# Attention on one core: the score matmul is issued before the matmul of the maximum pass in each sub-slot

## What is computed

```python
qkv = x @ attn_qkvw + attn_qkvb              # x is the layernormed input
scores = jnp.einsum('bhqd,bhkd->bhqk', q, k) * scale
probs = jax.nn.softmax(scores, axis=-1)
ctx = jnp.einsum('bhqk,bhkd->bhqd', probs, v)
```

## Time and profile before

| | |
|---|---|
| median of 3 timed runs | 3867.29 us |
| the three runs | 3867.56, 3867.29, 3861.1 us |
| time of the profiled execution | 3863.99 us |
| span of its trace | 3862.3 us |
| busy share of the span: PE, DVE, ACT, POOL | 86%, 63%, 45%, 43% |
| granted TensorE clock, mean | 0.952 |

### The profile page before, as it was taken

One profiled execution on the slowest core, in us unless ns is written; L12 is line 12 of the kernel. 1 busy time (PEld: TensorE's weight loads), 2 busy tenths in 40 slices (PEclk: granted clock), 3 DMA queues, 4 the chain that ended last, 5 costly groups with the idle time before them and its releaser, 6 DMA issues. The chain is left out here.

```text
span 3862.3 us, 66576 instructions
## 1 busy us (share of the span) xinstructions
PE 3336.4 (86%) x25168; PEld 1740.8 (45%) x25168; DVE 2434.6 (63%) x4416; ACT 1739.6 (45%) x2240; POOL 1644.3 (43%) x1785
## 2 busy tenths in 40 slices
PE   0899999999999999999994899967888887856999
PEld 0344444444444444444442455533455444433444
DVE  8366666666666666666777666666676666653222
ACT  3266666666666666666665222211333333330000
POOL 2366666666666666666663122212322222230000
PEclk9999999999999999999997999988898998977999
DMA  4111111111111111111114445441122222114433
GB/s 163 30 45 40 45 41 47 42 47 48 39 45 42 47 42 49 45 39 36 39 39 150 143 161 171 159 175 61 60 88 88 82 77 88 66 49 169 157 147 119
DMA packets 197996, 310.93 MB, mean 81 GB/s; under 512 B 32320, under 2 KB 147008, under 8 KB 196288
## 3 DMA queue, kind: packets, MB, share of 16 engines
q1 hardware_dynamic: 193024, 290.06, 22.7%
q10 hardware_dynamic: 4608, 16.78, 1.1%
q0 software_dynamic: 64, 0.01, 0.0%
HBM read 151.53 MB, written 104.86 MB: 66 GB/s over the span
## 5 line engine op out<-in xcount | busy, mean ns | idle before, releaser
L679 DVE TENSOR_REDUCE nmax<-ring_ps 128x1 f32<-128x512 f32 x1024 | 686.9, 688 | 371.8 <-PE ring_ps L509 346.2
L767 POOL TENSOR_TENSOR elo<-e,ehi 128x1024 f16<-128x1024 f32 x256 | 633.2, 2474 | 515.2 <-ACT ehi L631 514.9
L568 PE MATMUL proj_ps<-xnT,wqk 128*128 128x512 f16 x3072 | 750.3, 381 | 25.8 <-ACT stage L640 23.3
L629 ACT ACTIVATE e<-st_ps,exp_scale 128x1024 f32<-128x1024 f32 x512 | 569.8, 1113 | 340.7 <-PE st_ps L529 294.4
L631 ACT ACTIVATE ehi<-st_ps,exp_scale 128x1024 f16<-128x1024 f32 x512 | 569.7, 1113 | 226.4 <-PE ctx_ps L549 226.4
L568 PEld LDWEIGHTS proj_ps<-xnT,wqk 128*128 128x128 f16 x3072 | 293.8, 98 | 412.8 <-ACT stage L640 54.3
L1412 PE MATMUL f_ps<-wm,fxT 128*128 128x512 f16 x1536 | 366.3, 395 | 43.2 <-DVE x L1623 28.5
L546 PE MATMUL ctx_ps<-v_sb,ehi 128*128 128x65 f16 x4096 | 374.5, 193 | 27.1 <-DVE sums L712 19.8
L529 PE MATMUL st_ps<-qs,ks 98*128 98x512 f16 x1024 | 391.5, 382 | 0.7 <-ACT ehi L631 0.6
L509 PE MATMUL ring_ps<-ks,qs 96*128 96x512 f16 x1024 | 388.3, 379 | 1.6 <-DVE nmax L679 1.3
L546 PEld LDWEIGHTS ctx_ps<-v_sb,ehi 128*128 128x128 f16 x4096 | 298.4, 97 | 184.0 <-DVE sums L712 73.5
(11 more groups left out here) (221 smaller groups left out, 4464.1 us busy)
## 6 DMA issues: line engine op xcount, KB each, us to landing
x<-x_scratch SPq DMA_DIRECT2D x64, 512.0 KB, 4.4
qs<-qk_hl SPq DMA_DIRECT2D x768, 32.0 KB, 1.9
ks<-qk_hl SPq DMA_DIRECT2D x768, 32.0 KB, 1.9
ctx_scratch<-ctx SPq DMA_DIRECT2D x64, 256.0 KB, 2.5
ct<-ctx_scratch SPq DMA_DIRECT2D x32, 512.0 KB, 4.5
xb<-in_L_attn_a_x_dram SPq DMA_DIRECT2D x32, 512.0 KB, 4.4
x_scratch<-xb SPq DMA_DIRECT2D x32, 512.0 KB, 2.6
xT_scratch<-xT SPq DMA_DIRECT2D x32, 512.0 KB, 3.1
```

What stands on the lines that cost most here:

```text
L568: mm = pe.matmul(proj_ps[:], wqk[:, wp, c, H * qk + P * g:H * qk + P * g + P], xnT[:, b % 2, xp, c, :], start=(n == 0), stop=(n == 23))
L629: nc.scalar.activation(e32[:, half], st_ps[:, half], ACT.Exp, scale=exp_scale[:, 0:1]).then_inc(e32_done, 1)
L679: dve.tensor_reduce(nmax[:, h % 2, c:c + 1], ring_ps[:, ring_max(h, c) % 2, :], AX.X, ALU.max, negate=True).then_inc(ring_free, 1)
L767: nc.gpsimd.tensor_tensor(elo[:, h % 2, 2:4, :], e32[:, 1], ehi[:, h % 2, 2:4, :], ALU.subtract).then_inc(elo_pool, 1)
```

## The change

Two calls change places in TensorE's program of a sub-slot. Nothing else is touched: the same instructions, tiles and semaphores.

```diff
@@ -611,8 +611,8 @@
                             for c in range(T):
                                 if (s, c) in turns:
                                     turn(turns[s, c])
+                                scores(s, c)
                                 max_scores(s + 2, c)
-                                scores(s, c)
                                 for f in fills.get((s, c), []):
                                     unit(*f)
                                 if c == 1:
```

## The result

The changed kernel takes 3876.23 us (median of 8 runs, 3871.09 to 3880.94) against 3866.22 us before (8 runs, 3861.1 to 3868.51): 10.0 us slower, ratio 1.0027 with a 95% interval of 1.0017 to 1.0038. The forecast was 3873.7 us, 6.4 us over its base. The profiled execution took 3874.64 us with a span of 3872.9 us.

A forecast was written before the change was run, and what follows sets the result against it. TensorE, busy 1779.5 of 1895 us in the attention stage, was taken as the bound; 3.0 + 1.7 + 0 + 0.2 + 1.5 = 6.4 us on 3867.3 gave 3873.7 us. Own range 3869 to 3879 us; 8 in 10, 3863 to 3884.

The forecast's parts named there:

- The shift of 0.22 us: In each sub-slot the swap makes the scores 0.22 us earlier and the maximum pass 0.22 us later.
- Nothing from the earlier scores: TensorE's waits for ScalarE do not shorten: gain 0, bounds 0 and 25 us.
- Group ends with statistics: At 25 places VectorE's chain delays TensorE; L686 absorbs part, leaving 0.09 or 0.15 us each: 3.0 us.
- The first of these places: First group end with statistics: VectorE's L703 comes second to GpSimd's L767; costs 1.7 us, bounds 0 and 1.95.
- Group ends without statistics: At 27 group ends, 0.40 us of cover takes up the 0.22 us: cost 0.
- The last batch: Seven group ends without a turn; L703 is held by GpSimd's L824 anyway: 0.2 us, bounds 0 and 1.5.
- The last slots: Slots without projection, a loop through VectorE: 0.22 us longer per round, 7 rounds, 1.5 us, bounds 0 and 2.2.
- Slower or the same: Chances for the whole launch: slower by over 0.2% 0.40, within 0.2% 0.52, faster 0.08.
- The waits on ScalarE "about 20 us" after: Sign in the profile after: TensorE's waits for ScalarE stay at 53.7 and about 20 us.
- Rival 1: At 25 group ends with statistics L767 beats VectorE's L703: 47 us in place of 3.0, 3918 us; chance 0.12.
- Rival 2: L686 absorbs nothing; 0.22 us paid in full at 26 + 7 + 7 and more places: 3877 us; chance 0.13.
- rivals 3 and 4: Third: nothing measurable, 0 to 2 us, 3868 us, chance 0.12. Fourth: earlier scores shorten ScalarE waits, 3842 us, chance 0.07.

The follow-up runs named there:

- e5: Kernel before, with the new order only in sub-slot 15 of the groups up to slot 207 (52 sub-slots): 3871.0 us against 3868.6 us, ratio 1.0004.
- e8: Changed kernel (new order everywhere) with the statistics on VectorE one sub-slot earlier: 3866.3 us, ratio 0.9994 to the kernel before.
- e3: Changed kernel plus three unread 512-column matmuls in each of sub-slots 0 and 1 of slots 248 to 253: 3868.7 us, ratio 1.0001 to the kernel before.
- e2: Kernel before, with the new order only in the last slots (242 on): 3875.4 us, ratio 1.0016.
- e4: Kernel before (old order) plus three unread 512-column matmuls in each of sub-slots 0 and 1 of slots 248 to 253: 3864.5 us, ratio 0.9991.
- e11: Kernel before, unchanged, executed once more for a second trace: 3868.43 us.
- e6: Changed kernel plus one tiny one-column VectorE memset, without a wait, just ahead of L703 at group ends with statistics: 3885.2 us (5 runs).

## Why the prediction was right, and where it was not

- **The shift of 0.22 us.** Right: in each pair at the full clock L509 starts 0.22 us behind L529. The Trainium skill, page "TensorE: Matmul & The Clock Gate", section "Back-to-back issue gap", gives about 131 ns for 512 columns in such a stream. The traces do not agree: an estimate from it is 0.13 us per slot in the last slots, and the two kernels with added matmuls there show 0.22.
- **Nothing from the earlier scores.** Right: 53.7 us before and after.
- **Group ends with statistics, 3.0 us.** Right: 3.07 us, absorbed by L686 as worked out, and e5 shows that no other sub-slot of this stretch takes part. (L686 did not find GpSimd done, as the prediction has it, but started 0.05 us before L824's end; it was not held.)
- **The first of these places, 1.7 us.** The size is right (1.74 us), the way there only in part: L689 was held by L824 first, by 0.85 us, and this had not been seen. L703 was therefore held for less, 2.18 us long in place of the "about 3 us" of the signs. The working also speaks of "a held L703" in the earlier trace rows; the held one there is GpSimd's L767, which needed 1.98 us from the end of a free L703. That changes nothing in the 2.1 us.
- **Group ends without statistics, 0.** Right, and shown again by e8.
- **The last batch, 0.2 us.** 0.07 us; L686 is held there, and L703 ends with L824 as before.
- **The last slots, 1.5 us.** This is the step that failed. The 0.22 us per round are right (5.23 against 5.01 us at full clock), but the step that put the rounds at the full clock was wrong. The trace of before already had a granted clock of 0.87 there, and I used rows taken at 1.00 only. In the new order the clock falls for 41 us, and a round costs 6.5 us. The term was 7.5 us, five times what I said, and outside its bounds of 0 and 2.2. With the clock kept up (e3) 1.3 us of it are left, near the 1.5 of the prediction; the other 6.2 us are the clock, to which the prediction gave no term. Why the clock stays down is open.
- **The sum.** 6.4 us forecast, 10.0 measured by the medians and 10.65 in the two traces. In the traces 3.07 + 1.74 + 0.07 in the body and 7.5 in the last slots make 12.4, and the remaining -1.7 lie before slot 2 and in later stages, where traces of one kernel differ by more than that. So the forecast came as close as it did partly by luck: the stretches that it speaks of lost nearly twice the 6.4 us.
- **Slower or the same.** I gave 0.52 to no change beyond 0.2% and 0.40 to slower; it was slower, by 0.27% (0.17 to 0.38). By the chances as listed the two come to about 0.54 and 0.38. With the last slots at their true price the balance would have been the other way.
- **The waits on ScalarE "about 20 us" after.** Wrong: 12.8 us. I had not looked at sub-slot 3, where L689 now starts 0.19 us behind GpSimd's L824 of the turn and before started 0.02 us ahead of it (1174.26 against 1174.28). It cost nothing only because another wait was there to be used up.
- **Rival 1**, VectorE losing the race. It did not happen in the changed kernel, but it was near: at a lead of 0.02 us. Pushed 0.22 us further it costs 60.6 us, against 47 us in the rival: 44.3 us are the lost races, 1.77 us each in place of 1.9, and the rest is a fallen clock behind ten of them, which the rival did not have. The Trainium skill's rule on the port pair (page "SBUF — State Buffer", section "Who interferes with whom") is that whoever comes first holds it and the other is blocked. The traces agree in the outcome: the winner runs its full length (1.22 us for L703, 2.13 us for L767) and the other ends a fixed time after it (L703 1.08 us, L767 1.98 us). They do not quite agree on who comes first, since VectorE won with a start up to 0.02 us behind. Rival 2, the shift in full, is refuted by e5, and rivals 3 and 4 by the measured time and the unchanged 53.7 us.

## What to carry to other kernels

In this kernel a move of 0.22 us in the order of one engine cost nothing at some places, 0.09 to 0.22 us at others and 1.7 us where a race was lost, depending on what else ran at that moment on VectorE and GpSimd, which hold each other up. So before such a move, list the places where a chain runs without slack, and for each the distance to the next start on the other engine. Look at a stage's ramp-down separately from its body: the loop there can have another limit, and here the granted clock was 0.87 and then 0.53 where the body had 1.00. And a wait that grows in the table is a loss only if the next wait does not shrink by the same amount.

## What was not expected of the hardware

- VectorE wins with a start up to 0.02 us behind GpSimd's (at the first place with statistics in five traces: before, e2, e4, e5 and e11; L703 is 1.22 us long in each), and loses at 0.03 us behind (e6, L703 3.18 us long). If the border is the same at all places, it lies in a span of about 0.01 us; the losing side is one case.
- The order of two matmuls, with no change in the amount of work, goes with a granted clock that stays down for 41 us. At full clock TensorE is idle for 1.7 us of 5.0 in a slot of the old order (before) and 1.8 of 5.2 in the new one (e2); at the lower clock it is idle for only 0.9 us of 6.5, and yet the clock stayed down. Why is open, and e2, with the same order in the last slots, had its clock back sooner. What e3 shows is that 36 matmuls that nobody needs can pay for themselves: 6.2 us in the traces and 7.5 in the medians in the new order. In the old order (e4) the traces show 1.2 us, and a gain of the launch is not clear of noise.
- A VectorE memset of one column before L703 moved it by 0.006 us, and one of 88 columns with a wait on its end by 0.22 us.
